# Flamingo layer on one core: who sums which output rows at the end, and in what order plane 1 is loaded

## The reference

```
x   = x + tanh(g_xattn) * attention(h(x), ctx)
out = x + tanh(g_ffn) * ffn(h(x))

ffn(y): scores = sigmoid(y @ W_router);  top 2 of (scores + bias), weights normed to sum 1
        shared = (silu(y @ Wg_s) * (y @ Wu_s)) @ Wd_s
        routed = sum over the 2 chosen experts e of weight * ((silu(y @ Wg[e]) * (y @ Wu[e])) @ Wd[e])
        shared + routed
```

## Time and profile before

| | us |
|---|---|
| median of three runs | 305.68 |
| lowest and highest | 304.5, 306.01 |
| span of the profiled execution | 304.1 |
| TensorE busy | 274.8 |
| VectorE busy | 239.4 |
| GpSimd busy | 172.6 |
| ScalarE busy | 160.7 |

### The profile page before, as it was taken

The page is one execution under the profiler, slowest core; times in us unless marked ns, Lnnn a source line. Parts: engine busy times, 40 slices in busy tenths (PEclk is TensorE's granted clock), DMA queues, the critical chain, the costliest instruction groups (busy, mean ns, idle before and its releaser), DMA issues.

```text
span 304.1 us, 6562 instructions
## 1 busy us (share of the span) xinstructions
PE 274.8 (90%) x1746; PEld 246.3 (81%) x1747; DVE 239.4 (79%) x691; ACT 160.7 (53%) x414; POOL 172.6 (57%) x234
## 2 busy tenths in 40 slices
PE   2899989999999999999996668988799999999994
PEld 1788767998897898999886657877699899999883
DVE  0489989899899789899989565479877777777684
ACT  1452475656666566564453433654455555566731
POOL 8012225777758886897855876648544344444430
PEclk9999999999999999999999999999999999999999
DMA  6999994123359999923121122323343434446796
GB/s 185 361 288 314 306 293 140 41 77 100 103 167 302 312 286 318 270 69 106 35 70 56 59 81 90 105 56 86 90 118 111 123 96 122 121 114 167 249 325 232
DMA packets 45006, 49.74 MB, mean 164 GB/s; under 512 B 3928, under 2 KB 41650, under 8 KB 44978
## 3 DMA queue, kind: packets, MB, share of 16 engines
q1 hardware_dynamic: 39938, 39.37, 45.5%
q0 software_dynamic: 3408, 8.46, 8.1%
q10 hardware_dynamic: 1632, 1.57, 1.5%
HBM read 21.67 MB, written 28.64 MB: 165 GB/s over the span
## 4 chain that ended last, share of the span: by engine, by line
PE 60%; DVE 24%; issue 8%; ACT 4%; DMA 2%; SPq 1%; ACTq 0%; DVEq 0%
PE bank L1401 7%; PE bank L1403 6%; PE bank L1402 5%; PE scores_ps L1401 5%; PE scores_ps L1403 4%; PE scores_ps L1402 4%; DVE row_max L1146 3%; DVE probs L1152 3%; DVE row_sum L1136 3%; PE bank L1347 3%; DVE pT_lo L1129 3%; PE scores_ps L1438 2%; PE bank L1598 2%; DMA Wq_sb<-in_L_xattn_Wq_dram 2%; PE bank L1438 2%
## 5 line engine op out<-in xcount | busy, mean ns | idle before, releaser
L699 POOL DMA_INDIRECT routed_dram<-probs,sct_idx x39 | 38.1, 977 | 49.3 <-ACT probs L911 46.8
L649 POOL TENSOR_TENSOR probs<-probs,row_inv 128x1024 f32<-128x1024 f32 x16 | 30.5, 1909 | 26.4 <-DVE row_inv L1140 26.3
L613 POOL DMA_INDIRECT rows_dram<-xn,slot_i x32 | 32.0, 1000 | 14.0 <-issue 10.5
L1401 PE MATMUL bank<-AB_hi,pT_hi 128*128 128x256 f32 x128 | 37.0, 289 | 2.4 <-DVE pT_lo L1129 2.4
L1403 PE MATMUL bank<-AB_hi,pT_lo 128*128 128x256 f32 x128 | 35.8, 279 | 0.0
L1402 PE MATMUL bank<-AB_lo,pT_hi 128*128 128x256 f32 x128 | 35.7, 279 | 0.0
L768 ACT ACTIVATE probs<-probs 128x1024 f32<-128x1024 f32 x16 | 17.0, 1061 | 29.5 <-DVE probs L1152 25.4
L1401 PE MATMUL scores_ps<-AB_hi,xnT_hi 128*128 128x512 f32 x64 | 27.0, 421 | 2.5 <-DVE xnT_lo L1122 2.3
L1401 PEld LDWEIGHTS bank<-AB_hi,pT_hi 128*128 128x128 f32 x128 | 24.1, 188 | 3.0 <-issue 2.9
L1403 PE MATMUL scores_ps<-AB_hi,xnT_lo 128*128 128x512 f32 x64 | 25.3, 395 | 0.0
L1402 PE MATMUL scores_ps<-AB_lo,xnT_hi 128*128 128x512 f32 x64 | 25.3, 395 | 0.0
(11 more groups left out here) (248 smaller groups left out, 876.6 us busy)
## 6 DMA issues: line engine op xcount, KB each, us to landing
rows_dram<-pad_rows SPq DMA_DIRECT2D x10, 1040.0 KB, 16.5
rows_dram<-pad_rows SPq DMA_DIRECT2D x8, 780.0 KB, 12.2
AB_free<-routed_dram SPq DMA_DIRECT2D x8, 512.0 KB, 6.4
probs<-rows_dram SPq DMA_DIRECT2D x30, 130.0 KB
raw_buf<-in_L_ffn_Wg_dram SPq DMA_DIRECT2D x8, 192.0 KB, 2.5
raw_buf<-in_L_ffn_Wu_dram SPq DMA_DIRECT2D x8, 192.0 KB, 2.6
out_dram<-x_sb ACTq DMA_DIRECT2D x6, 256.0 KB, 2.9
pT_hi<-rows_dram SPq DMA_DIRECT2D x9, 130.0 KB
```

The costliest lines, as they stand in the source:

```text
L613: nc.gpsimd.indirect_dma_start(rows_dram[:, :], bass.IndirectOffsetOnAxis(ap=slot_i[:, t, k:k + 1], axis=0), xn2[:, t % KEEP, :], None).th ...
L649: nc.gpsimd.tensor_tensor(pr, pr, row_inv[:, :].unsqueeze(2).to_broadcast([P, H, KV]), ALU.mult).then_inc(norm_done, 1)
L699: nc.gpsimd.indirect_dma_start(routed_dram[:, :], bass.IndirectOffsetOnAxis(ap=sct_idx[(k - 2) % (2 * RING)][:, 0:1], axis=0), y_sb[ks][:, ...
L1401: nc.tensor.matmul(out_ap, a_hi, b_hi, start=first, stop=False)
```

## The change

- Tiles 8 to 11 leave VectorE. For each plane ScalarE scales the loaded rows in place (`scale_low`, `scale_high`: plane * weight), and GpSimd adds them to `x_sb` (`add_low(t)`, `add_high(t)`). ScalarE's low copies and GpSimd's low adds of tiles 8 and 9 stand in step 39 of the expert loop, which is `j == SLOT_TILES`. ScalarE's copies of tiles 10 and 11 stand in step 40; GpSimd's adds of these tiles follow the loop.
- TensorE's four products of the x rows with the identity go; when `late_ps[z]` has both planes, VectorE adds it to `x_sb` (`tail_added`), and ScalarE's four copies go.
- VectorE's order becomes low 0, low 1, high 0, the four tail adds, high 1.
- Plane 1 is loaded in the order 0, 2, 3, 1.
- Stores: ScalarE's queue issues pairs 0, 1, 4, 5, 3; SP issues 6, 7, 2.

```diff
+BY_TWO = range(8, 12)
+HIGH_ORDER = (0, 2, 3, 1)
@@ sync
-                for c in range(T // PLANE):
-                    n = k * (T // PLANE) + c
+                for n, c in enumerate(HIGH_ORDER if k else range(T // PLANE), k * (T // PLANE)):
...
-            for c in range(4, NB // 2):
-                sp.wait_ge(plane1_added, 2 * (c + 1))
+            for c in (6, 7):
+                sp.wait_ge(tail_added, 2 * (c - 6) + 2)
                 store(sp, c)
+            sp.wait_ge(plane1_added, 6)
+            store(sp, 2)
@@ gpsimd
+            def add_low(t):
+                n = t - BY_TWO[0] + 1
+                pool.wait_ge(plane0_scaled, n)
+                nc.gpsimd.tensor_tensor(x_sb[:, t, :], plane[0][:, t, :], x_sb[:, t, :], ALU.add).then_inc(pool_low_added, 1)
+            def add_high(t):
+                n = t - BY_TWO[0] + 1
+                pool.wait_ge(plane1_scaled, n)
+                pool.wait_ge(pool_low_added, n)
+                nc.gpsimd.tensor_tensor(x_sb[:, t, :], plane[1][:, t, :], x_sb[:, t, :], ALU.add).then_inc(pool_high_added, 1)
...
+                if isinstance(j, int) and j == SLOT_TILES:
+                    pool.wait_ge(late_added, NB)
+                    add_low(BY_TWO[0])
+                    add_low(BY_TWO[1])
             expert_loop(pool, expert_step)
+            add_low(BY_TWO[2])
+            add_low(BY_TWO[3])
+            for t in BY_TWO:
+                add_high(t)
@@ scalar
+            def scale_low(t):
+                act.wait_ge(plane0_loaded[t // PLANE], 16)
+                nc.scalar.activation(plane[0][:, t, :], plane[0][:, t, :], ACT.Copy, scale=weight[:, t, 0:1]).then_inc(plane0_scaled, 1)
+            def scale_high(t):
+                act.wait_ge(plane1_loaded[t // PLANE], 16)
+                nc.scalar.activation(plane[1][:, t, :], plane[1][:, t, :], ACT.Copy, scale=weight[:, t, 1:2]).then_inc(plane1_scaled, 1)
...
+                if isinstance(j, int) and SLOT_TILES <= j <= SLOT_TILES + 1:
+                    for t in BY_TWO[2 * (j - SLOT_TILES):2 * (j - SLOT_TILES) + 2]:
+                        scale_low(t)
             expert_loop(act, expert_step)
             late_hidden(NB + 3)
-            for c in range(4):
-                act.wait_ge(plane1_added, 2 * (c + 1))
+            for t in BY_TWO[0:2]:
+                scale_high(t)
+            act.wait_ge(plane1_added, 2)
+            store(act, 0)
+            for t in BY_TWO[2:4]:
+                scale_high(t)
+            act.wait_ge(plane1_added, 4)
+            store(act, 1)
+            for c in (4, 5):
+                act.wait_ge(pool_high_added, 2 * (c - 4) + 2)
                 store(act, c)
-            for z in range(NB, T):
-                act.wait_ge(tail_summed, z - NB + 1)
-                nc.scalar.activation(x_sb[:, z, :], late_ps[z][:, 0:D], ACT.Copy).then_inc(tail_copied, 1)
-                if z % 2:
-                    act.wait_ge(tail_copied, z - NB + 1)
-                    store(act, z // 2)
+            act.wait_ge(plane1_added, 8)
+            store(act, 3)
@@ vector
-            for c in range(NB // PLANE):
-                if c:
-                    add_low(c)
+            def add_high(c):
                 dve.wait_ge(plane1_loaded[c], 16)
...
+            add_low(1)
+            add_high(0)
+            for z in range(NB, T):
+                dve.wait_ge(tail_summed, z - NB + 1)
+                nc.vector.tensor_tensor(x_sb[:, z, :], late_ps[z][:, 0:D], x_sb[:, z, :], ALU.add).then_inc(tail_added, 1)
+            add_high(1)
@@ tensor
-            for z in range(NB, T):
-                tail_sum(z, ident[:, :], x_sb[:, z, :])
```

More of the change, by code:

```diff
@@ L277, in flamingo_layer @@
         tail_summed = sem("tail_summed")
-        tail_copied = sem("tail_copied")
+        tail_added = sem("tail_added")
         chunk_turns_done = sem("chunk_turns_done")
         plane0_added = sem("plane0_added")
+        plane0_scaled = sem("plane0_scaled")
+        plane1_scaled = sem("plane1_scaled")
+        pool_low_added = sem("pool_low_added")
+        pool_high_added = sem("pool_high_added")
         plane1_added = sem("plane1_added")
```

## The result

| us | before | changed |
|---|---|---|
| median of 18 runs each | 305.45 | 308.0 |
| lowest and highest | 303.52, 307.1 | 305.43, 309.45 |
| profiled execution's span | 304.1 | 304.2 |

The ratio is 1.0089, with a 95% interval of 1.0065 to 1.0112: some 2.7 us slower. The forecast, no change that can be measured, is wrong; from the median of 305.68 that it started from, the ratio gives 308.4, outside its range. The mechanism that I thought likeliest, VectorE and GpSimd taking turns, is there and nearly as large as I put it. A second one, GpSimd's exit, is not in my sum.

What follows compares the result with a forecast made beforehand. Two chains ending together (VectorE 300.13, TensorE with ScalarE's copies 300.25), then the stores, were taken to bound the kernel. The last landing at 304.45 against 303.7 added 0.75 to 305.68, giving 306.4; range 305.0 to 308.0.

Steps and rivals of the forecast that it cites:

- VectorE and GpSimd taking turns: In the end phase, adds with SBUF inputs exclude each other one instruction at a time: GpSimd ready near 300.3, VectorE 301.9.
- ScalarE's copies of tiles 10 and 11 hold TensorE up by 0.90: Two copies ahead of the last `late_hidden`, 0.45 each and without cover, make TensorE's tail start 0.90 later (0.56 to 0.98).
- x rows off TensorE: Four products of 0.433 us leave TensorE's tail, taking 1.73 us away there.
- plane 1 in another order: Loading plane 1 as 0, 2, 3, 1 costs no waits; cover is gone if the fourth load lands 2.7 later.
- A: Main case, chance 0.47: the two engines' adds alternate, VectorE ends at 301.9, median 306.4 (305.8 to 307.2).
- B: Rival, chance 0.25: VectorE's overlapping scaled adds shut GpSimd out until 294.5; GpSimd ends near 303.05, time 307.8.
- C: Rival, chance 0.20: no exclusion of any weight; VectorE ends at 300.89, change -0.5 to 0, time 305.4.
- One to three us of idle time ahead of the tail adds: VectorE was to idle this long after `add_high(0)`, waiting for TensorE's tile 12 before the tail adds.
- Last store issued at 301.95, landed at 304.45: ScalarE's queue issues the last pair, tiles 6 and 7, after VectorE; landing takes 2.5 us, +0.75 against 303.7.
- the span ends 0.4 later: At the program's end, the profiled span was taken to close 0.4 us after the last store lands.

Runs made afterwards that it cites:

- the run with the copies behind: Changed kernel with ScalarE's plane 0 copies of tiles 10 and 11 moved behind the last `late_hidden`: ratio 1.0085 (1.0049 to 1.0121).
- operand from PSUM: Changed kernel with VectorE's last twelve scaled adds taking their second operand from a PSUM bank instead of `x_sb`: ratio 1.0041 (1.0008 to 1.0073).
- two tiles on GpSimd: Changed kernel with only tiles 8 and 9 on ScalarE and GpSimd, tiles 10 and 11 back on VectorE, stores reordered: ratio 1.0043 (1.0011 to 1.0075).
- a last fill of 0.10 us: Kernel before plus a one-column GpSimd fill after VectorE's sixth (early) or twelfth (late) plane 1 scaled add: ratio 1.0009 early, 1.0081 late.
- the candidate: Kernel before with TensorE's tail made tile by tile and plane 1 loaded in order 0, 3, 1, 2: ratio 1.0019 (0.998 to 1.0057).

## Why the prediction was wrong, point by point

Moments of after are given in coordinates of before, 2.24 added.

- **ScalarE's copies of tiles 10 and 11 hold TensorE up by 0.90: right in kind, 0.71 in size.** The pair at L913 starts at 290.52 after, the last `late_hidden` 0.80 later. The first products of TensorE's tail, in the timelines of before, after and the run with the copies behind, start 5.36, 6.07 and again 5.36 after the first scaled add (the chain of the earlier trace rows, from which I counted, has those of before at 294.39):

```profile
294.23 0.60 PE L1442 MATMUL bank<-x_sb,ident 128*128 128x256 f32 x2
```

```profile
292.70 0.60 PE L1493 MATMUL bank<-AB_free,late_hid 128*128 128x256 f32 x2
```

```profile
295.56 0.60 PE L1495 MATMUL bank<-AB_free,late_hid 128*128 128x256 f32 x2
```

- **x rows off TensorE: 1.73 us less there, held (1.72); plane 1 in another order: the waits cost nothing, held.** TensorE's tail takes 3.62 where it took 5.34. The kernel without GpSimd's adds, which keeps both parts, gives 1.0014.
- **VectorE and GpSimd take turns: held, A over B and C.** Single adds that meet are long on both sides (0.90 to 0.98 in the rows above), they end in alternation, and no wait of over 1.5 us stands in front of one. GpSimd's end was put at 300.3 and is 298.11 + 2.24 = 300.35; VectorE's at 301.9 and is 301.43, after a hold-up of 2.49 - 1.67 = 0.82 in `add_high(1)`, where I had 0.7 to 1.4. The operand from PSUM takes the exclusion away, so it is shown and not only argued.
- **One to three us of idle time ahead of the tail adds: too much.** It is 0.45. `add_low(1)` and `add_high(0)` took 5.62 together instead of 3.26, and ate it. It is 2.78 once the exclusion is gone.
- **Last store issued at 301.95, landed at 304.45: held.** Issued at 301.46, landed after 2.7 (2.5 predicted) at 304.16, against 303.7 before. By the stores alone the change costs 0.5 us (0.75 predicted), within no change.
- **"the span ends 0.4 later": this step failed.** The 0.4 of the earlier trace rows was read as a constant behind the last landing. It is what is left when the slowest engine's exit is earlier than that landing. I let GpSimd's part end with its last add, with the words "Nothing stands behind it in the queue but the adds"; the drain stands behind it, 5.88 us. By the sum's own number, 300.3 + 5.9 is 306.2, where I let the span end at 304.85; with it the forecast of the same case would have been 306.2 + 1.6 = 307.8. The row was there to read in the trace of before: a drain at 293.5 of 7.49, 2.7 us short of the last landing. By that row GpSimd's last instruction may end up to about 294.7 + 2.7 = 297.4 before it costs anything, and my own GpSimd sum passed that even undisturbed (299.37).

So the 2.3 us of the traces are 0.5 of later stores and 1.8 of exit. Divided by cause they overlap: the exclusion makes GpSimd's end later as well as VectorE's. Without it, 1.1 of 2.3 go (operand from PSUM); the rest, 1.2, is mostly the exit behind adds at their own pace, 1.0 beyond its usual 0.4. Rival B's 307.8 lies near the measured time by accident: it had GpSimd shut out until 294.5 and ending at 303.05, and neither is in the trace.

What stays open: what GpSimd does in the 5.9 us wasn't tried. Nor was the exit taken away with all eight adds kept: with two tiles on GpSimd half of them went as well. It is not settled either whether a tail made tile by tile gains a few tenths.

## What to carry to other kernels

Price work given to GpSimd near the end of a program to the end of its drain and not to that of its last instruction: here some 6 us more, free only while the last stores land later. Before giving VectorE's adds to GpSimd, look whether both sides read two operands from SBUF; here eight adds of 0.72 cost VectorE's twelve 3.2 us (2.62 + 3.07 + 2.49 against three times 1.67), nearly all of what the eight scaled adds taken off it are worth (two batches at 1.59). When the chain of waits stops well before the span does, read the last rows of every queue.

## What was not expected of the hardware

- GpSimd's drain at the end of the program ends some 5.9 us after a last add (5.88 with the change) and after a last fill of 0.10 us, whether that stood early or late, and 6.1 to 6.6 after a last scatter (6.3 before, 6.55 without adds on GpSimd, 6.1 in the candidate). VectorE's ends 0.08 after its last add.
- Two streams of adds with two inputs in SBUF each go by turns here: under GpSimd's adds a batch of four scaled adds of 1.67 becomes 2.49 to 3.07, and a pair of GpSimd adds of 1.43 becomes 1.81 to 1.85. Neither stream runs through before the other starts.
